# Two changes to TensorE's order in a two-layer vision block: attention without the unread matmuls, pairs of expert tiles transposed one tile sooner

## The reference

```
x = x + window_attention(_ln_c(x))        # 16 heads of 8 channels, windows of 64 tokens, dilated 2x2, rotary
t = t + moe0(_ln_t(t))                    # 8 experts, top 2, silu(x w1) * (x w3), then w2
x = x + group_whitening(_ln_c(x))         # covariance per group of 32 channels, 3 Newton steps
t = t + moe1(_ln_t(t))                    # 8 experts, top 2, each with biases, silu gate, w2
```

## Time and profile before

| | |
|---|---|
| time, median of 3 runs | 941.62 us (930.8 to 943.98) |
| profiled execution, its own time | 927.54 us |
| its span | 925.7 us |
| busy: PE, DVE, ACT, POOL | 69%, 49%, 38%, 46% |
| mean granted TensorE clock | 0.867 of full speed |
| unread matmuls (L1150), all uses | 484, busy 106.0 us |

### The profile page before, as it was taken

The page is one execution under the profiler, slowest core; times in us unless marked ns, Lnnn a source line. Parts: engine busy times, 40 slices in busy tenths (PEclk is TensorE's granted clock), DMA queues, the critical chain, the costliest instruction groups (busy, mean ns, idle before and its releaser), DMA issues.

```text
span 925.7 us, 17267 instructions
## 1 busy us (share of the span) xinstructions
PE 641.8 (69%) x5696; PEld 448.8 (48%) x5696; DVE 450.1 (49%) x1258; ACT 349.4 (38%) x859; POOL 422.2 (46%) x417
## 2 busy tenths in 40 slices
PE   2778888888878575664988884885444667678770
PEld 1245555545445454553556553664333545556550
DVE  1576776955775343312334335647525352344434
ACT  1455655435343342332445442314123422234430
POOL 3354553554545255566233342102776445644440
PEclk9889999989888796777899997999676876899995
DMA  7000299996000111222323205000153413235307
GB/s 268 29 13 13 50 174 162 172 164 107 13 14 24 45 42 52 55 64 82 103 78 104 95 26 178 5 1 1 40 76 70 86 44 99 81 82 97 79 29 272
DMA packets 81206, 73.76 MB, mean 80 GB/s; under 512 B 9263, under 2 KB 70840, under 8 KB 80736
## 3 DMA queue, kind: packets, MB, share of 16 engines
q1 hardware_dynamic: 71792, 54.51, 28.1%
q0 software_dynamic: 8896, 17.47, 5.8%
q10 hardware_dynamic: 432, 0.68, 0.2%
HBM read 35.37 MB, written 38.16 MB: 79 GB/s over the span
## 4 chain that ended last, share of the span: by engine, by line
PE 27%; issue 15%; DVE 6%; POOL 4%; another core or an unknown queue 3%; ACT 3%; DMA 2%; POOLq 0%; DVEq 0%; ACTq 0%; SPq 0%
PE bank L1297 7%; PE bank L1282 5%; PE bank L1284 3%; PE bank L1283 3%; PE bank L1289 2%; POOL region L627 2%; PE bank L1330 2%; DMA fetched<-results 1%; POOL X L595 1%; DVE xl L914 1%; DVE X L961 1%; PE bank L1150 1%; PE bank L1264 1%; PE bank L1332 1%
## 5 line engine op out<-in xcount | busy, mean ns | idle before, releaser
L613 POOL DMA_INDIRECT results<-work,rowbuf x142 | 138.0, 972 | 198.5 <-ACT work L755 85.0
L920 DVE SCALAR_TENSOR_TENSOR work<-work,rowbuf,bank 128x256 f32<-128x256 f32 x142 | 68.2, 480 | 190.9 <-ACT work L745 147.4
L1282 PE MATMUL bank<-Wh,xl 128*128 x142 | 76.6, 539 | 87.2 <-DVE xl L914 36.2
L1297 PE MATMUL bank<-W,work 128*128 x568 | 103.2, 309 | 25.7 <-ACT work L750 11.4
L1297 PEld LDWEIGHTS bank<-W,work 128*128 128x128 f32 x568 | 90.9, 213 | 61.0 <-issue 52.4
L1150 PE MATMUL bank<-half 128*128 128x384 bf16 x484 | 106.0, 366 | 13.2 <-DVE X L891 8.5
L745 ACT ACTIVATE work<-bank 128x256 f32<-128x256 f32 x142 | 54.6, 384 | 147.7 <-PE bank L1284 79.3
L1282 PEld LDWEIGHTS bank<-Wh,xl 128*128 128x128 f32 x142 | 29.9, 211 | 109.9 <-issue 109.8
L627 POOL DMA_INDIRECT region<-rows_a,where x64 | 63.3, 989 | 22.3 <-issue 19.5
L1150 PEld LDWEIGHTS bank<-half 128*128 128x128 bf16 x484 | 50.5, 108 | 46.6 <-issue 15.9
L750 ACT ACTIVATE work<-bank 128x256 f32<-128x256 f32 x142 | 54.3, 382 | 25.1 <-PE bank L1289 10.3
(11 more groups left out here) (230 smaller groups left out, 1231.0 us busy)
## 6 DMA issues: line engine op xcount, KB each, us to landing
region<-pad SPq DMA_DIRECT2D x16, 1040.0 KB
rowbuf<-region SPq DMA_DIRECT2D x142, 65.0 KB
fetched<-results SPq DMA_DIRECT2D x16, 512.0 KB, 4.5
spare<-w1gv_dram SPq DMA_DIRECT2D x8, 640.0 KB
spare<-b_dram SPq DMA_DIRECT2D x71, 64.0 KB
results<-work,rowbuf POOLq DMA_INDIRECT x142
work<-w_dram SPq DMA_DIRECT2D x8, 256.0 KB, 2.8
W<-w_dram SPq DMA_DIRECT2D x2, 1024.0 KB, 12.1
```

Of the source, the lines that this page charges most:

```text
L613: pool.indirect_dma_start(results[layer], bass.IndirectOffsetOnAxis(ap=at, axis=0), ysb[:, T % YRING, :], None, bounds_check=PAIRS - 1, oo ...
L920: v.scalar_tensor_tensor(out=hh[:, i % 2, :], in0=sg[:, i % 2, :], scalar=rowbuf[:, i % RING, GATE_AT:GATE_AT + 1], in1=bank[:, b, FF:2 * FF],
L1282: mm(bank[:, b, :], low, wh, start=True, stop=False)
L1297: last = mm(bank[:, b, 0:P], hT[:, i % 2, ft * P:(ft + 1) * P], W2[layer][:, bass.ds(experts[i] * FT + ft, 1), :].rearrange("p a n -> p (a ...
```

## The change

The call of warm in front of the transpositions of attention goes, and its constant with it. All other calls of warm stay. In tile_steps the transposition of a pair gets the number two ahead of the pair's first tile and not one ahead, except for the first pair of a layer, which keeps its place. ScalarE's xh and VectorE's xl carry the same name and move with it. This holds in both layers.

```diff
-WARM_PIECE, WARM_BLOCK, WARM_CHAIN = 8, 6, 3
+WARM_BLOCK, WARM_CHAIN = 6, 3
...
         if t % 2 == 0:
-            yield at[t] - 1, "xt", layer * PAIRS_MOE + t // 2
+            yield max(at[t] - 2, at[0] - 1), "xt", layer * PAIRS_MOE + t // 2
         yield at[t], "up", T
...
             if name == "PT":
                 b = pe_claim(name, i)
-                warm(b, WARM_PIECE)
                 pe.wait_ge(p_nrm, i + 1)
```

## The result

The changed kernel takes 897.38 us (median of 4 executions, 894.15 to 899.67). The kernel before took 927.28, 930.8, 941.62 and 943.98 us on the same chip, and since some executions of it are slow ones, all ratios here compare fast executions with fast ones, though the times given are medians of all. The ratio is 0.9657, 95% interval 0.9592 to 0.9722: faster by 32 us (26 to 38) where 73 were forecast. The profiled execution of the changed kernel took 899.67 us, the slowest of its four, that of the kernel before 927.54 us, one of its fastest. Their spans are 897.9 and 925.7 us, so the two profiles differ by only 27.8 us.

The account below looks back on a forecast made before the run. The prediction took TensorE as the bound, the engine the others follow in attention and waiting for xl in the tiles. Attention's 30 us plus the tiles' 43 made 73 us off the 941.6 us median: 868 us predicted, range 843 to 912.

Parts of the forecast that it names:

- the third of the things that take some back: Attention: without bursts the clock stays low longer, taking back 11 us of the gain, bounds 0 and 85 us.
- I take half, 12 us: Tiles beside puts: the earlier transpositions gain 12 us, between bounds of nothing and 26 us.
- The bursts' price: Attention: removing the stretch's 29 bursts saves 46.4 us, 50.2 us together with those outside it.
- I take the low share as 35% in place of 18%: Attention: share of time at the low clock after removal; 37 us more low time, of which 11 us are lost.
- the clock stays low: Rival: clock low throughout attention, which loses 44 us while tiles gain 43; 942.6 us, no change; chance 0.08.
- 112 us at 1.00, in which TensorE did other work: Attention: argument against the low-clock rival, that full clock held for 112 us with TensorE mostly on other work than bursts.
- At 53 us S ran low although TensorE had no pause: Attention: reading of the earlier trace, used to say it agrees only in part with the rule that activity keeps the clock.
- VectorE's chain and O: Attention: longer waits for VectorE's rotation take back 7 us, and O's waits without a shown releaser 2 us.
- the third rival: Attention gains nothing because VectorE's chain from J to the rotation sets the pace; some 895 us; chance 0.13.
- The steady tiles: Tiles without puts: the wait for xl before up ends, gaining 31 us, bounds 26 and 33.
- The second rival: Tiles: the move gains nothing because dn or ScalarE's copies take the wait's place; some 908 us; chance 0.14.
- Late rows: Rival in the tiles: TensorE waits at a pair's head for rows not yet in; 961 us or more; chance 0.05.

Follow-up runs that it names:

- run 3: Kernel before with sixteen instead of eight unread matmuls ahead of each piece's transpositions in attention: 967.34 us, ratio 1.0393 to the kernel before.
- run 2: Kernel before with only the pairs' transpositions moved one tile ahead, the bursts kept: 911.86 us, ratio 0.9751 to the kernel before.
- run 1: Kernel before with only the bursts ahead of PT removed, the pairs at their old place: 935.08 us, ratio 0.9994 to the kernel before.
- run 5: Changed kernel with six unread matmuls put into TensorE's waits ahead of O and ahead of Q or K: 882.55 us, ratio 0.9459 to the kernel before.
- run 7: Changed kernel with eight instead of four buffers for rows of results: 898.45 us, ratio 0.9639 to the kernel before.
- run 8: Changed kernel without half of layer 1's puts (a second expert's rows), results filled with zeros at the start instead: 870.7 us in one profile.

## Why the prediction was right and wrong

The direction and the range (843 to 912) held; the gain was 32 us and not 73, less than half. The step that failed is the third of the things that take some back, the clock: 11 us were taken and 37 measured. Next comes "I take half, 12 us" beside the puts, where the waits did not get shorter at all. Of the chain of steps:

**The bursts' price held.** 46.4 us were forecast for the 29 of the stretch and 47.0 measured from start to start; run 3 measures the same price from the other side, 2.60 us for sixteen.

**The clock term failed.** "I take the low share as 35% in place of 18%", at 0.40 x 0.75 per us, gave 11 us. The low time between 55 and 309 us went from 41 to 120 us, from 16% to 47%, 79 us more and not 37 (62 more against run 2, which has the bursts too). That is the larger error. And a low us cost 37/79 = 0.47 us, not 0.30. The price was taken from S alone, which the lower level slows less than the transpositions and Q. And TensorE was taken as busy for three quarters of the low time: it is busy for 82% of it (103.8 of the 126.5 low us between 55 and 318), and the bursts, which had filled part of the low time, are gone from it; the earlier trace rows had shown 8.84 of 10 us busy at a clock of 0.50. The bound of 85 us held. The rival "the clock stays low" has the right mechanism at less than half its size: 37 of its 85 us.

As to what holds the clock, "112 us at 1.00, in which TensorE did other work" was read as a sign that the bursts were not needed. Run 1 shows that they were: the same stretch at 0.84 without them. A second reading was wrong. "At 53 us S ran low although TensorE had no pause" overlooks two: TensorE stood still for 1.31 us ahead of PT at 49.26 and for 1.29 us ahead of O at 51.64, and the clock's record turns low at 51.9 (kernel before):

```profile
49.26 1.09 PE L1201 MATMUL bank<-C,Sx 128*128 128x128 f32 x8 [1.31 <-POOL Sx L587]
51.64 1.78 PE L1215 MATMUL bank<-PT,Vm 64*32 64x64 f32 x64 [1.29 <-issue]
```

The Trainium skill's page TensorE: Matmul & The Clock Gate, section on the HAM clock gate, warns of pauses, frequent short ones between groups of matmuls too. The trace agrees with that better than the prediction had it: besides the two above, matmuls put into pauses of 1.1 us won 38 us of low time back (run 5). But from 146.50 to 152 us the kernel after ran at the lower level through S, J and PT without a pause (the last one, 1.16 us, had ended at 144.64).

**VectorE's chain and O: the sum right, by luck.** 7 and 2 us were taken for waits that grow, and the idle time of the stretch grew by 10 us. But the wait for the rotation, for which the 7 stood, went from 2.0 us in front of the bursts to 3.0 in front of PT (L1200 above). O's went from 25.8 to 29.0, and Q's wait for ScalarE's copy, in no term, from 13.4 to 17.5 (L1170). The 3.0 us are far from the 15 that would have meant the third rival. That rival's time, 895 us, is nearly what was measured, but run 3 rules out its cause: bursts lay on the path, VectorE's chain did not hide them.

So attention is 47 - 37 - 10 = 0 us between the two profiles, 0 by run 1, and some 10 us at the most by runs 2 and 7, where 30 were forecast.

**The steady tiles: right mechanism, 23.4 us in place of 31.** The wait for xl is gone, a pair takes 3.47 us (forecast under 3.6). All idle time of TensorE fell from 14.4 to 1.4 us between up 30 and 70, so layer 0 came nearly as forecast. Between up 103 and 141 it fell from 17.1 to 6.8 us, of which 5.7 stand in front of dn: four result buffers became too few for the faster pace, and with eight (run 7) it is 3.5 us. Some 2 us of the forecast's 33.4 lie outside these tiles.

**Beside the puts: the step "I take half, 12 us" failed**, by its own doubt. The bound from below, nothing, was right for the waits: all idle time of TensorE between up 2 and 30 was 41.0 us and is 40.7, between up 71 and 103 33.0 and 33.5. The 6.2 us gained are matmuls that took less time, 72.4 to 68.1 and 75.0 to 72.9 us busy (in the first of these stretches the low time fell from 61 to 50 us), which no step forecast. ScalarE and VectorE stood still for want of TensorE's signal, and that hits whichever instruction of TensorE comes next. With xl early, up ran in their shadow and dn waited. At the end of layer 0's puts TensorE had waited 2.93 us for xl and then 6.79 ahead of dn; now it waits once (kernel after):

```profile
435.88 1.22 PE L1296 MATMUL bank<-W,work 128*128 x4 [12.01 <-ACT work L750]
```

Runs 2, 7 and 8 show that neither the place of the transpositions nor buffers set that pace, but the number of puts. The second rival, dn in the place of xl, came true here, and for 5.7 us in the steady tiles of layer 1.

**Late rows** did not occur: after the first pair L1263 has no idle time.

## What to carry to other kernels

An unread matmul in front of work is a loan: read the whole of the work beside it at both clock levels before calling it waste, and price the lower level over the mix of operations, not over one. Where such matmuls hold the clock, put them into waits that are there anyway (0.9459 against 0.9657), rather than removing them or leaving them on the path. A price is read from start to start, not from busy time. And a wait that begins because several engines stand still at once is not shortened by moving one of its instructions; it turns up in front of the next.

## What the runs showed of the hardware that was not expected

TensorE's clock stayed at the lower level through 6 us of S, J and PT without a pause, and came back in O (157.39 us, changed kernel) with no burst near. Records of matmuls overlap: 326 ns is one's duration, 0.16 us its share of a row of sixteen. And while GpSimd issued indirect transfers 1.28 us apart, TensorE's semaphores were raised up to 12.0 us after the recorded ends of its matmuls, while those that ScalarE and VectorE raise were never more than 1 us late.
